# One empty gather ahead of the first tile's, and the last output tile's residual added by TensorE

## The reference

```python
x = x + _L0_xattn_ref(_layernorm(x), ctx_1024, Wq, Wkv, Wout, bout)   # ... out @ Wout + bout
x = x + _L0_ffn_ref(_layernorm(x), Wg, W1, W2)

# in _L0_ffn_ref:
    logits = xt @ Wg
    probs = softmax(logits)                       # 2048 tokens, 8 experts
    _, top_idx = top_k(probs.T, T // E)           # each expert picks its 256 best tokens
    tok2exp = where(assigned, argmax(masked), argmax(probs))
    for e in range(E):
        gate = where(tok2exp == e, weights, 0)
        out = out + gate[:, None] * (gelu(xt @ W1[e]) @ W2[e])
```

## Time and profile before

| | us |
|---|---|
| median of three runs (lowest, highest) | 372.68 (372.06, 373.13) |
| the profiled execution's own time | 371.51 |
| its span, first to last instruction | 369.5 |
| busy in the span: PE, PEld, DVE, ACT, POOL | 350.9, 224.8, 207.4, 264.4, 126.3 |

### The profile page before, as it was taken

The page is one execution under the profiler, slowest core; times in us unless marked ns, Lnnn a source line. Parts: engine busy times, 40 slices in busy tenths (PEclk is TensorE's granted clock), DMA queues, the critical chain, the costliest instruction groups (busy, mean ns, idle before and its releaser), DMA issues.

```text
span 369.5 us, 11056 instructions
## 1 busy us (share of the span) xinstructions
PE 350.9 (95%) x4371; PEld 224.8 (61%) x4371; DVE 207.4 (56%) x711; ACT 264.4 (72%) x386; POOL 126.3 (34%) x222
## 2 busy tenths in 40 slices
PE   8999999999999999999999999998786799999995
PEld 7757547444434444444434344787665799999994
DVE  4999797454546455454635456697785233333332
ACT  3675564999999999999999999307851445555440
POOL 6445768001010313131120306504404346555523
PEclk9999999999999999999999999999999899999999
DMA  7634899505366563826565125401652321323200
GB/s 246 192 106 138 248 249 324 175 4 150 73 197 159 186 171 92 249 45 179 129 180 126 35 35 182 134 2 64 217 179 63 103 86 58 110 70 93 70 26 33
DMA packets 37374, 47.83 MB, mean 129 GB/s; under 512 B 8780, under 2 KB 26626, under 8 KB 37313
## 3 DMA queue, kind: packets, MB, share of 16 engines
q1 hardware_dynamic: 34368, 40.26, 37.3%
q0 software_dynamic: 2608, 6.43, 5.6%
q10 hardware_dynamic: 337, 0.32, 0.3%
HBM read 32.84 MB, written 13.81 MB: 126 GB/s over the span
## 4 chain that ended last, share of the span: by engine, by line
PE 79%; ACT 9%; DVE 7%; issue 3%; POOL 1%; POOLq 0%; ACTq 0%
PE ps L1189 20%; PE ps L1165 18%; PE ps L1412 10%; PE ps L1426 9%; PE ps L1143 8%; ACT pbuf L912 7%; PE ps L1089 4%; DVE stats L1794 1%; PE ps L1058 1%; ACT v_st L962 1%; PE ps L1400 1%; DVE xe L1789 1%; PE ps L1282 1%; POOL pbuf L789 1%; PE ps L1072 1%
## 5 line engine op out<-in xcount | busy, mean ns | idle before, releaser
L912 ACT ACTIVATE pbuf<-ps 128x948 f32<-128x948 f32 (+2 forms) x192 | 167.5, 1028 | 0.1
L1758 DVE SCALAR_TENSOR_TENSOR pbuf<-pbuf,seen 128x128 f32<-128x128 f32 (+1 forms) x256 | 70.9, 309 | 65.6 <-ACT pbuf L912 64.8
L1165 PE MATMUL ps<-q_st,k_st 98*32 98x512 bf16 (+4 forms) x1920 | 100.0, 328 | 1.5 <-ACT pbuf L912 1.4
L1189 PE MATMUL ps<-pbuf,v_st 128*32 128x512 f32 (+4 forms) x1024 | 96.4, 472 | 0.0
L1165 PEld LDWEIGHTS ps<-q_st,k_st 98*32 98x32 bf16 x1920 | 46.8, 96 | 68.5 <-issue 27.2
L1412 PE MATMUL ps<-mid,piece_f 128*128 128x128 f32 x320 | 40.5, 281 | 4.0 <-issue 4.0
L758 POOL TENSOR_TENSOR mid<-mid 64x256 f32<-64x256 f32 x28 | 20.3, 752 | 69.0 <-DVE pbuf L1751 50.9
L1412 PEld LDWEIGHTS ps<-mid,piece_f 128*128 128x128 f32 x320 | 40.2, 198 | 5.1 <-issue 4.2
L1189 PEld LDWEIGHTS ps<-pbuf,v_st 128*32 128x32 f32 x1024 | 27.3, 109 | 25.3 <-issue 10.5
L1426 PE MATMUL ps<-pbuf,mid 128*128 128x256 f32 (+1 forms) x168 | 37.7, 369 | 0.0
L999 ACT ACTIVATE mid<-ps 128x512 f32<-128x512 f32 x20 | 11.9, 597 | 34.8 <-issue 18.0
(11 more groups left out here) (274 smaller groups left out, 388.0 us busy)
## 6 DMA issues: line engine op xcount, KB each, us to landing
wts<-in_L_ffn_W SPq DMA_DIRECT2D x16, 512.0 KB, 5.6
k_st<-k_cut SPq DMA_DIRECT2D x48, 147.2 KB, 3.3
q_st<-q_cut SPq DMA_DIRECT2D x48, 128.0 KB, 3.2
q_cut<-wts SPq DMA_DIRECT2D x8, 384.0 KB, 4.6
k_cut<-wts SPq DMA_DIRECT2D x8, 384.0 KB, 4.9
token_rows<-xe SPq DMA_DIRECT2D x4, 512.0 KB, 4.4
mid<-mid SPq DMA_DIRECT2D x28, 64.0 KB, 2.5
mid<-reciprocals SPq DMA_DIRECT2D x28, 64.0 KB, 2.3
```

What stands on the lines that cost most here:

```text
L912: nc.scalar.activation(pbuf[:, s % 2, r, c0:end], st_ps[(s * GH + r) % NST][:, c0:end], ACT.Exp, scale=SCALE).then_inc(exp_done, 1)
L1165: last = nc.tensor.matmul(st_ps[(s * GH + r) % NST][c:c + 32, a:z], k_st[pa][:, r, t * P + c:t * P + c + 32], q_st[pa][:, r, q0 + a - c0:q ...
L1189: last = nc.tensor.matmul(o_ps[32 * r:32 * r + 32, a:z], v_st[pa][:, t, r, :], pbuf[:, s % 2, GH - 1 if t == SHORT else r, a + dc:z + dc], ...
L1758: last = nc.vector.scalar_tensor_tensor(a, a, 3.0e38, seen[:, off:off + w], ALU.min, ALU.mult)
```

## The change

The diff has two parts that don't touch each other.

The first is on POOL. A new index column `no_rows` is filled with 4096, one above the last half row of `token_rows` (the bound is 4095). When `rows_sent` is complete, POOL issues a gather of the same shape as the first tile's with these indices into `y_sb[0]`. All 128 lie out of bounds, so it moves no row; its completion still counts up `none_in`. The first tile's gather follows as before. DVE waits for `none_in` before it first writes `y_sb[0]`.

The second is on the last of the 16 output tiles. PE adds the residual itself: ahead of the two products it multiplies the identity with the tile's `xe` (264 columns) into the same bank. DVE takes the statistics from PSUM (`stats2_last`), without `x1_row`. ACT copies the 8 logits out of PSUM as soon as the statistics are read, and the 256 columns of the row behind the exponential. The last `tops` moves behind the add of EPS, since it needs the copied logits.

```diff
             pool.wait_ge(pv_done, 2 * NG * NSTEP + 2)
+            nc.gpsimd.iota(no_rows[:, :], pattern=[[0, 1]], base=T * XW // D, channel_multiplier=0).then_inc(none_made, 1)
...
+            pool.wait_ge(none_made, 1)
             pool.wait_ge(rows_sent, 16 * 2 * (TT // 4))
+            pool.sem_inc(index_there, 1)
+            pool.indirect_dma_start(y_sb[0], None, rows_d.rearrange("t (h d) -> (t h) d", d=D),
+                                    bass.IndirectOffsetOnAxis(no_rows[:, 0:1], 0),
+                                    bounds_check=pair_end, oob_is_err=False).then_inc(none_in, 16)
             pool.sem_inc(index_there, 1)
             pool.wait_ge(first_done, 1)
...
+            last_t, last_ps = WTILES[TT - 1], bank(WBANK[TT - 1])
+            act.wait_ge(x1_done, TT - 1)
+            act.wait_ge(last_stats_done, 1)
+            nc.scalar.copy(xe[:, last_t, D:D + E], last_ps[:, D:D + E]).then_inc(x1_done, 1)
             act.wait_ge(mean2_done, TT)
...
             nc.scalar.activation(r_probs, r_probs, ACT.Exp).then_inc(lexp_done, 1)
+            nc.scalar.copy(xe[:, last_t, 0:D], last_ps[:, 0:D]).then_inc(last_row_done, 1)
+            act.wait_ge(last_row_done, 1)
...
+                if n == TT - 1:
+                    nc.tensor.matmul(bank(WBANK[n])[:, 0:D + E], ident[:, :], xe[:, t, :], start=True, stop=False)
                 for k in range(KT):
                     last = nc.tensor.matmul(bank(WBANK[n])[:, 0:D + E], pk[:, b, k, at:at + P], wout_sb[:, k, :],
-                                            start=(k == 0), stop=(k == KT - 1))
+                                            start=(k == 0 and n < TT - 1), stop=(k == KT - 1))
...
+            def stats2_last(n):
+
+                v.wait_ge(wo_ready, n + 1)
+                nc.vector.bn_stats(stats[:, WTILES[n], :], bank(WBANK[n])[:, 0:D]).then_inc(last_stats_done, 1)
+                v.wait_ge(last_stats_done, 1)
+                nc.vector.bn_aggr(mv[:, WTILES[n], :], stats[:, WTILES[n], :]).then_inc(mean2_done, 1)
...
-            for n in range(6, TT):
+            for n in range(6, TT - 1):
...
+            mean2(TT - 3)
             mean2(TT - 2)
-            tops(WTILES[12], WTILES[15] + 1)
-            mean2(TT - 1)
+            stats2_last(TT - 1)
             v.wait_ge(mean2_done, TT)
             seq(nc.vector.tensor_scalar_add(ve[:, :], mv[:, :, 1], EPS))
+            v.wait_ge(x1_done, TT)
+            tops(WTILES[12], WTILES[15] + 1)
             count(nc.vector.reciprocal(nt1[:, :], ve[:, :]))
...
+                if k == 0:
+                    v.wait_ge(none_in, 16)
```

More of the change, by code:

```diff
@@ L318, in xattn_ffn @@
         x1_done = sem("x1_done")
+        last_stats_done = sem("last_stats_done")
+        last_row_done = sem("last_row_done")
         xn2s_done = sem("xn2s_done")
@@ L362, in xattn_ffn @@
         first_in = sem("first_in")
+        none_made = sem("none_made")
+        none_in = sem("none_in")
         fx_ready = sem("fx_ready")
@@ L507, in xattn_ffn @@
         first_tok = sb("first_tok", [P, 1], U32)
+        no_rows = sb("no_rows", [P, 1], U32)
         slot_gate = sb("slot_gate", [P, NS])
```

## The result

| | before | after |
|---|---|---|
| median, us (lowest to highest; 6 runs each, side by side) | 372.6 (371.9 to 373.13) | 375.29 (374.2 to 377.78) |
| ratio of after to before, 95% interval | | 1.0094 (1.0068 to 1.012) |
| profiled execution, us | 371.51 | 375.15 |
| its span, us, and mean granted clock | 369.5, 0.993 | 373.1, 0.987 |

The changed kernel is slower by 0.9%, above the range of the prediction. Everything ahead of the first tile's transposes went nearly as forecast; what grew is the hold, the time between the end of those transposes and the start of their readers.

A forecast was written before the change was run, and what follows sets the result against it. PE holds 79% of the chain; the change can win only where it leaves PE or stands still. -0.02 for the tile and 0 for the gather: 371.51 to 371.5 profiled, 1.17 more as median, 372.6 us; range 367.0 to 373.6.

The forecast's parts named there:

- The last output tile: Last of the output tiles: DVE saves what PE's added product costs; term -0.02 us, bounds -0.1 and +0.45.
- The empty gather, on POOL: POOL ahead of the first tile's gather: starts about 277.1, over by 278.4, at most 1.29 us long, costs nothing.
- could be a price of first use ... I take 0: POOL's first gather: its extra 0.25 us might be paid by the empty one; bounds 0 and -0.25, taken as 0.
- The hold: Between the first tile's transposes and their readers: 3.8 us nothing shown accounts for; forecast keeps readers at 288.2.
- 0 for the gather: The empty gather's term in the sum: neither gain nor cost, 0 us.
- Rival 1: Behind the first tile's gather: the empty gather pays for the hold, -4.9 to -5.2 us, 367.5; chance 0.28, whole or part.
- Rival 2: PE's slot products: each gathering start holds PE, up to 3.8 us, 376.5, if over one product is due; chance 0.11.
- Rival 3: DVE's chain work beside the empty gather: POOL holds DVE for a whole gather, +1.25 us, 373.9; chance 0.04.

The follow-up runs named there:

- e2: Kernel before with only the last output tile's edits, no empty gather: 370.92 us against 371.72, ratio 0.9991.
- e4: Kernel before with PE's filler matmuls 512 columns wide instead of 128, a quarter as many: 367.08 us against 371.72, ratio 0.9883.
- e5: Kernel before with an empty gather of half-length rows of x, some 42 us ahead of the first tile's: 365.81 us against 366.52, ratio 0.9988.
- e6: Kernel before with the change's empty gather and 512-column fillers: 365.52 us against 366.52, ratio 0.9973.
- e8: Kernel before with 512-column fillers only at the last three places (36, 6 and 6 short ones): 365.87 us against 366.52, ratio 0.9983.
- e14: Same kernel as e5, run again: kernel before with an early empty gather, 366.63 us against 366.77, ratio 0.9995.
- e1: Kernel before with the empty gather alone, without the last output tile's edits: 374.85 us against 371.72, ratio 1.0088.
- e3: Kernel before with five of the burst's six gathers kept until the first tile's transposes are over: 367.95 us against 371.72, ratio 0.9894.
- e11: Changed kernel with a second empty gather right behind the first: 375.55 us, kernel before 372.15, ratio 1.0101.
- e18: Same kernel as e5, a third time: kernel before with an early empty gather, 375.64 us against 372.68, ratio 1.0074.
- e13: Changed kernel with five of the burst's six gathers kept until the first tile's transposes are over: 366.67 us, kernel before 366.77, ratio 0.9996.
- e16: Changed kernel with 512-column fillers and five burst gathers kept until the first transposes are over: 365.68 us, kernel before 366.77, ratio 0.9987.
- e7: Kernel before with 512-column fillers and five burst gathers kept until the first transposes are over: 365.68 us against 366.52, ratio 0.999.
- e15: Same kernel as e7, run again: kernel before with wide fillers and delayed burst, 365.63 us against 366.77, ratio 0.9982.

## Why the prediction was wrong

**The last output tile** was right: -0.02 was forecast for the tile, -0.08 came, and all its hidden pieces stayed hidden. e2's 0.9991 (0.9965 to 1.0016) agrees, but can't tell so little from nothing.

**The empty gather, on POOL**: time and place were right (277.1 forecast, 277.48 measured, over by 278.98 where I had 278.4; it took 1.50 and not 1.29, and was free). The step "could be a price of first use ... I take 0" failed: it was 0.25, as the bound had it. The row of 1.29 misled me, since a gather beside a DVE copy is long for a reason of its own: in e4, e5, e6, e8 and e14 the gather of the burst that starts beside DVE's two weight copies takes 1.31 to 1.40 and the others 1.00 (e5: 1.40 from 286.09, the copies from 285.90). POOL held DVE nowhere. These 0.25 us brought nothing, for `fx_ready` was counted up late for another reason. (Of the about 6 us of code loading that the Trainium skill has for the first call of a freshly loaded kernel, in "GPSIMD Engine Reference", section 2.1 "Instruction dispatch", no trace here shows more than these 0.25. Nor does one show the lock of the Trainium skill's page "SBUF — State Buffer", section "Who interferes with whom", with DVE as the one held: DVE wrote `first_tok` 30.53 us behind ACT's square root in both kernels, beside 1.50 us of gather.)

**The hold** is where the forecast fell, and the step that failed is the term "0 for the gather". I had written that nothing shown accounts for the hold, and yet summed as though it were a constant that either stays or goes: the term had bounds of -0.25 and +1.25, and neither took in that a thing with no known cause can grow. In its place the hold alone measured +3.02 us, and the gather alone (e1) 1.0088 of the kernel before, some 3.1 us. I also took the 3.8 us for one fixed wait. By the table above it is a wait with a fixed end, 8.9 us behind the burst's start, ahead of which the kernel before still gets its first release through, and the changed kernel doesn't. The only rows of before that bore on it were those of the earlier trace rows: it stood beside a burst of gathers on POOL, while PE, ACT and DVE waited. An edit that adds one more gather should have had the size of the hold itself as its bound, upward as well as downward.

**Rival 1** (an empty gather pays for the hold) had the wrong cause: the first use is paid and the hold is longer. That all would be won by removing the hold was sized about right; e4 and e3 gave 4.6 and 3.8 us where it had 4.9 to 5.2. **Rival 2** (each start of gathering holds PE) had the sign and, by luck, nearly the size, 376.5 against 375.29; its place was wrong: it set the second hold in the slot products behind the empty gather, where there was none, and e11 and e18 show that neither the number nor the place of empty gathers matters. The point from which it was to decide never came up. **Rival 3** did not happen.

**What stays open**: why a gather made earlier, even 42 us earlier, keeps the first transposes' release from getting through; whether PE or its report is held; what sets the two levels; and whether the hold exists in a run that isn't recorded. Not in doubt is that the loss is the hold: by the trace nothing else grew, and where there was no hold, the kernels with an empty gather (e5, e6, e13, e14, e16) stood within 0.3% of the kernel before. The changed kernel as it is was never run there. Nor was one run with the index column and the semaphores but without the gather.

## What to carry to other kernels

A stall that the profile can't attribute is not a constant: give any edit on the engines or queues beside it the whole stall as a bound in both directions. Find the cause before trying to win it: here two edits of a few lines, aimed at what stood beside the stall (a burst of gathers, a stream of short filler matmuls), each won over 1% where the stall existed, and in the combinations that were run without it (e6, e7, e13, e15, e16) they cost nothing. On the changed kernel with the stall only the fillers were tried, and they won back the loss and 0.2% more. And run the kernel before beside every candidate, on more than one occasion: its own level moved by 1.7% here (366.52 to 372.68), more than any of the edits.

## What the runs showed of the hardware

- While POOL issues a burst of indirect gathers, the semaphore that a transpose counts up can be counted up to 6.8 us behind the transpose's (modelled) end; its readers start 0.02 us later. In ten of the twelve traces with such a delay the last held readers went free 8.6 to 8.9 us behind the burst's first gather.
- The hold comes and goes for the same kernel on one chip (e14 and e18, 366.63 and 375.64 us).
- The first indirect gather of a run takes 0.25 us more on POOL: the first tile's 1.25 as the first (before) and 1.00 behind an empty one (after), an empty one 1.49 as the first and 1.26 as the second (e11).
- A gather that starts beside a DVE copy takes up to 0.4 us more (1.31 to 1.40 in e4, e5, e6, e8 and e14, beside 1.00).
- Fillers of 512 columns keep the clock as well as four times as many of 128: the mean granted clock was 0.998 to 1.000 with them in e4, e6, e7, e15 and e16, and 0.997 to 1.000 with the short ones, without a hold, in e5, e13 and e14.
